# Mamba and mixture-of-experts layer on one core: the experts' rows are gathered plain and added by TensorE, where the gathering DMA added them before

## The reference

```python
x = L0_attn_x
xn = _layernorm(x)
x = x + attn(xn) + moe(xn)

# attn, for each direction (the backward one on the reversed sequence):
delta = softplus(dt @ dt_w.T + dt_b);  A = -exp(A_log)
h = h * exp(delta[..., None] * A) + (delta * xi)[..., None] * B[:, None, :]   # step by step over 512 tokens
y = einsum('bdn,bn->bd', h, C);  y = (y + xi * D) * silu(z);  out = y @ out_w.T
# moe, for the expert e that a token's router picks (argmax of 8 logits):
ye = (silu(xe @ gate_w[e].T) * (xe @ up_w[e].T)) @ down_w[e].T
```

## Time and profile before

| what | value |
|---|---|
| median of 3 runs | 995.46 us (993.8 to 995.51) |
| the profiled execution's own time | 996.43 us |
| its span, first to last instruction | 994.3 us |
| mean granted TensorE clock | 0.892 of full speed |
| busy: PE, DVE, ACT, POOL | 822.7, 889.1, 701.4, 817.0 us |
| POOL busy in 200 to 300, 600 to 700, 800 to 850, 900 to 950 us | 95.28, 88.43, 47.70, 47.70 us |
| DVE busy in 200 to 300, 600 to 700, 800 to 850, 900 to 950 us | 87.81, 92.22, 50.00, 40.84 us |
| ACT busy in 800 to 850, 900 to 950 us | 31.01, 26.02 us |

### The profile page before, as it was taken

One profiled execution on the slowest core, in us unless ns is written; L12 is line 12 of the kernel. 1 busy time (PEld: TensorE's weight loads), 2 busy tenths in 40 slices (PEclk: granted clock), 3 DMA queues, 4 the chain that ended last, 5 costly groups with the idle time before them and its releaser, 6 DMA issues.

```text
span 994.3 us, 10532 instructions
## 1 busy us (share of the span) xinstructions
PE 822.7 (83%) x2923; PEld 326.5 (33%) x2923; DVE 889.1 (89%) x622; ACT 701.4 (71%) x1167; POOL 817.0 (82%) x451
## 2 busy tenths in 40 slices
PE   5769886876869998989998998989998987676666
PEld 2223321132233543435343533435343321213112
DVE  4788979997899898999999897999989999895996
ACT  3877864746659789787998788788998584574440
POOL 0258767999999879897998878898888999999992
PEclk9778977797988999989999998989898897787779
DMA  6576262333273527464464626454453634634300
GB/s 193 155 200 177 54 183 54 143 88 92 102 187 138 131 65 217 117 192 112 148 173 144 138 76 202 121 173 128 142 151 85 156 59 124 141 115 95 69 1 11
DMA packets 93996, 125.54 MB, mean 126 GB/s; under 512 B 8042, under 2 KB 65771, under 8 KB 89843
## 3 DMA queue, kind: packets, MB, share of 16 engines
q1 hardware_dynamic: 88464, 120.15, 43.5%
q0 software_dynamic: 4736, 4.20, 2.1%
q10 hardware_dynamic: 738, 0.53, 0.2%
HBM read 77.53 MB, written 14.29 MB: 92 GB/s over the span
## 4 chain that ended last, share of the span: by engine, by line
PE 34%; POOL 29%; issue 17%; ACT 12%; DVE 3%; DMA 3%; SPq 1%; POOLq 0%; ACTq 0%; DVEq 0%
POOL hs L1250 18%; PE y L575 9%; PE front L513 6%; PE in_b L551 4%; POOL attn_in L1240 4%; POOL sorted_tokens L1221 3%; ACT dA L862 3%; ACT L871 3%; PE moe L696 2%; PE front L544 2%; PE front L526 2%; POOL yg L1212 2%; PE front L608 2%; PE moe L649 2%; PE moe L654 1%
## 5 line engine op out<-in xcount | busy, mean ns | idle before, releaser
L1250 POOL TENSOR_TENSOR hs<-hs,C_rep 128x1024 f32<-128x1024 f32 x252 | 595.4, 2416 | 123.0 <-DVE hs L1053 76.7
L862 ACT ACTIVATE dA<-delta_rep,A_sb 128x511 f32<-128x511 f32 x512 | 335.1, 715 | 66.3 <-DMA delta_rep<-tmpA 38.4
L1036 DVE TENSOR_TENSOR in_b<-in_b,B_rep 128x1024 f32<-128x1024 f32 x256 | 300.2, 1218 | 68.1 <-PE in_b L551 63.4
L575 PE MATMUL y<-hs,cst 128*32 128x512 f32 x1024 | 283.5, 681 | 46.7 <-POOL hs L1250 24.1
L1053 DVE TENSOR_TENSOR_SCAN hs<-dA,in_b 128x1024 f32<-128x1024 f32 x128 | 285.1, 2268 | 4.9 <-PE y L575 4.9
L1055 DVE TENSOR_TENSOR_SCAN hs<-dA,in_b 128x1024 f32<-128x1024 f32 x128 | 285.1, 2268 | 2.9 <-PE y L575 2.7
L551 PE MATMUL in_b<-du,cst 128*128 128x512 f32 x256 | 147.9, 662 | 24.7 <-DVE hs L1055 22.1
L513 PE MATMUL front<-xpad,w_in 128*128 128x512 f32 x248 | 124.9, 629 | 5.3 <-ACT zs L799 2.1
L575 PEld LDWEIGHTS y<-hs,cst 128*32 128x32 f32 x1024 | 53.5, 119 | 228.3 <-issue 177.7
L871 ACT ACT_TABLE_LOAD x73 | 93.7, 1283 | 14.1 <-PE moe L696 5.0
L544 PE MATMUL front<-dbc,w_dt 8*128 8x512 f32 x62 | 43.8, 792 | 37.3 <-ACT tmpB L825 19.4
(11 more groups left out here) (129 smaller groups left out, 771.6 us busy)
## 6 DMA issues: line engine op xcount, KB each, us to landing
delta_rep<-tmpA SPq DMA_DIRECT2D x126, 256.0 KB, 4.5
B_rep<-dbc_scratch SPq DMA_DIRECT2D x16, 1024.0 KB, 5.1
C_rep<-dbc_scratch SPq DMA_DIRECT2D x16, 1024.0 KB, 7.4
gu_w<-in_gate_up SPq DMA_DIRECT2D x39, 384.0 KB, 3.4
dn_w<-in_down SPq DMA_DIRECT2D x39, 192.0 KB, 2.5
xs<-sorted_tokens SPq DMA_DIRECT2D x39, 64.0 KB, 3.3
sorted_ffn<-ys SPq DMA_DIRECT2D x39, 64.0 KB, 1.6
sorted_tokens<-up_f SPq DMA_DIRECT2D x9, 256.0 KB, 4.1
```

What stands on the lines that cost most here:

```text
L575: i = e.matmul(Y[c * DD:(c + 1) * DD, :], sel, hs[:, (m + 2 * w + rh) % NH, r * L:(r + 1) * L], start=False, stop=(rh == 1 and r == RH - 1 ...
L862: i = e.activation(dA[:, m // 2 % NA, r * L + 1:(r + 1) * L], src, ACT.Exp, scale=A_sb[:, d, 2 * p + jj, r:r + 1])
L1036: e.tensor_tensor(to, in_b[:, 2 + 2 * odd, :].unsqueeze(1).broadcast_to([P, RH, L]), by, ALU.mult).then_inc(dve_mult, 1)
L1250: e.tensor_tensor(hs[:, m % NH, :], hs[:, m % NH, :], C_rep[:, u % 2, RH * rh:RH * rh + RH, :].rearrange("p r t -> p (r t)"), ALU.mult).th ...
```

## The change

For the sequences 0 to 5 the indirect DMAs no longer add. They write plain rows into half `b % 2` of `gu_w`, which the experts no longer need. TensorE puts the stored sum (`attn_in`) through the identity into the bank `M`, adds the gathered rows in the same way (`final_mm`, at step `g + 6`), and ScalarE copies `M` back into `attn_in` (at step `g + 7`), from where SP stores it as before (at step `g + 8`, now behind ScalarE's copy and not behind the gathers). GpSimd's gather no longer waits for the load of the stored sum, but from `b` = 2 on for the TensorE addition of `b - 2`.

```diff
+        def rows_of(b):
+
+            return gu_w[:, b % 2, :, :].rearrange("p a c -> p (a c)")[:, 0:KB * H].rearrange("p (k h) -> p k h", h=H)
+
...
                 for b in gathers(m, 8):
                     if b < NB - LATE:
-                        e.wait_ge(in_gather[b % 2], 64 * (b // 2 + 1))
+                        e.wait_ge(act_fin, b + 1)
                         e.dma_start(by_batch(out, b), attn_in[:, b % 2, :, :]).then_inc(out_fin[b % 2], 16)
...
+            def final_mm(b):
+
+                if b:
+                    e.wait_ge(act_fin, b)
+                else:
+                    e.wait_ge(act_ys, NTILE)
+                    e.wait_ge(act_up, NTILE)
+                e.wait_ge(in_attn[b % 2], 16 * (b // 2 + 1))
+                e.matmul(M[:, :], ident, attn_in[:, b % 2, :, :].rearrange("p k h -> p (k h)"), start=True, stop=False)
+                e.wait_ge(in_gather[b % 2], 64 * (b // 2 + 1))
+                e.matmul(M[:, :], ident, rows_of(b).rearrange("p k h -> p (k h)"),
+                         start=False, stop=True).then_inc(pe_fin, 1)
...
+                for b in gathers(m, 6):
+                    if b < NB - LATE:
+                        final_mm(b)
                 for c in norms(m, 5):
                     router(c)
...
+                for b in gathers(m, 7):
+                    if b < NB - LATE:
+                        e.wait_ge(pe_fin, b + 1)
+                        e.copy(attn_in[:, b % 2, :, :].rearrange("p k h -> p (k h)"), M[:, :]).then_inc(act_fin, 1)
...
                     if i < 0:
-                        e.wait_ge(in_attn[b % 2], 16 * (b // 2 + 1))
+                        if b >= 2:
+                            e.wait_ge(pe_fin, b - 1)
...
                         if i < 0:
-                            e.indirect_dma_start(out=attn_in[:, b % 2, k, :], out_offset=None, in_=ffn_d, in_offset=at,
-                                                 compute_op=ALU.add).then_inc(in_gather[b % 2], 16)
+                            e.indirect_dma_start(out=rows_of(b)[:, k, :], out_offset=None, in_=ffn_d,
+                                                 in_offset=at).then_inc(in_gather[b % 2], 16)
```

More of the change, by code:

```diff
@@ L248, in mamba_moe_kernel @@
         pe_first, pe_du, pe_y, pe_out = sem("pe_first"), sem("pe_du"), sem("pe_y"), sem("pe_out")
-        pe_base, pe_late = sem("pe_base"), sem("pe_late")
+        pe_base, pe_late, pe_fin = sem("pe_base"), sem("pe_late"), sem("pe_fin")
         pe_route, pe_xs, pe_gate, pe_up, pe_down = sem("pe_route"), sem("pe_xs"), sem("pe_gate"), sem("pe_up"), sem("pe_down")
@@ L258, in mamba_moe_kernel @@
         act_xsT, act_ys = sem("act_xsT"), sem("act_ys")
-        act_route = sem("act_route")
+        act_route, act_fin = sem("act_route"), sem("act_fin")
         act_y, act_D, act_up, act_out = sem("act_y"), sem("act_D"), sem("act_up"), sem("act_out")
```

## The result

The changed kernel takes 979.47 us (median of 5 runs, 977.51 to 980.77), the kernel before 994.55 us in the same comparison (5 runs). The ratio is 0.9839, with a 95% interval of 0.9826 to 0.9851, which is 16.0 us less (14.8 to 17.3); the two medians by themselves differ by 15.1 us. The forecast was 13.2 us less. So the direction and the place were right, and the size was short by some 3 us.

A forecast was written before the change was run, and what follows sets the result against it. GpSimd was taken as the bound from first gather to C(250): 14.2 us saved less 1 us of loss, 13.2 us, so 995.46 becomes 982.3 us. Range 979 to 990.5; its low end allowed 2 us for VectorE's tail or the clock.

The forecast's parts named there:

- What bounds it: From the first gather to C(250), about 180 us, GpSimd bounds the kernel while VectorE keeps up.
- The price of the adding, 14.2 us: On GpSimd, four adding gathers take 7.17 us, plain ones 4.80; the 2.37 us difference, times 6, is saved.
- I take 1 us of loss (bounds 0 and 3): Between 795 and 850 us GpSimd, running earlier, would wait for VectorE's scans, losing 1 us of the gain.
- So the tail ... moves by the full 14.2 us: The tail hangs on when GpSimd runs dry and moves 14.2 us earlier with it.
- behind each stand decay factors: ScalarE's six copies of 0.59 us delay only factors VectorE needs four steps later; cost 0.
- The wait at sequence 3: TensorE's second matmul waits for rows landing at 851.3; the sum starts 1.3 us later, VectorE's scans at 864.9.
- The wait at sequence 5: Rows land at 908.4, TensorE's second matmul ends at 910.5; VectorE loses 3 us, its later pair starts about 918.7.
- The slack at C(250): VectorE may start its pair by 920.0 without delaying GpSimd; estimated at 918.7, so 1.3 us remain.
- The end of C(251): VectorE's last multiplication ends about 954.6, again 1 us after GpSimd's last one.
- Rivals 1 and 2: VectorE becomes the bound, gain 5.4 to 10 us, chance 0.22; or final_mm holds TensorE at every gather, slower, 0.11.
- Rival 3: Gathers cost what they did, time 995 to 996 us; chance 0.05, shared with a stall just eating the gain.

The follow-up runs named there:

- Run 1: Changed kernel, but its gathers add again, onto the weights' buffer; matmuls, copy and waits kept. Ratio to the kernel before 0.9992.
- run 2: Kernel before with plain gathers onto attn_in, no new matmuls or copies, stored sum of sequences 0 to 5 lost. Ratio 0.9867.
- run 3: The change for sequences 0, 1 and 2 alone; 3, 4, 5 keep the adding DMA. Ratio to the kernel before 0.9936.
- Run 5: Kernel before with four unread identity matmuls filling TensorE's idle time ahead of the last sums of states. Ratio 0.9983.
- runs 3 and 4: The change for sequences 0, 1, 2 alone (ratio to the kernel before 0.9936), and for sequences 3, 4, 5 alone (0.9909).
- Runs 9 to 11: Changed kernel with VectorE gating y: three halves; six with additions at g + 8; six with additions at g + 6. Ratios 0.9844, 0.9888, 0.984.
- run 8: Changed kernel with TensorE's additions two steps earlier (g + 4) and ScalarE's copies at g + 5. Ratio to the kernel before 0.9913.

## Why the forecast was right in kind and short in size

**What bounds it: right.** In no profile of the two kernels does GpSimd wait for a scan between the first gather and C(250), and the two halves of the change shorten the middle part by 7.0 and 7.1 us, which add up to the whole.

**The price of the adding, 14.2 us: right.** 14.22 us measured in the middle part, blocks of four at 4.78 us where 4.80 were taken from the rows of another buffer. Run 1 shows that it is the adding.

**"I take 1 us of loss (bounds 0 and 3)": wrong, it was 0.** This is the first term that failed. I read the piece of 0.94 us called "issue" at 825.19 as a wait for a scan. It was none: the waits of GpSimd in the kernel before, in 788 to 968 us, name DMA issues alone. "Issue" in the chain is time in which the profile shows nothing to wait for; GpSimd was at work in it, since its records of five multiplications cover 814.57 to 826.74 without a break. After, the same five multiplications take 11.59 us, and no scan is late for them.

**"So the tail ... moves by the full 14.2 us": wrong by 1.6 us.** This is the larger of the two terms that failed, and it was missing from the sum rather than mis-sized: only the low bound of the range allowed 2 us for VectorE's tail or the clock, with no path worked out. The start of the tail moved as said, but its length did not stay. What the runs showed, over all profiles without filler: where VectorE came to C(251) about 4.2 us or more before GpSimd ran dry (before, run 2, run 3), TensorE idled for 3.6 to 4.6 us ahead of the last sums and these took 5.3 to 5.5 us. Where it came 0.2 to 2.2 us before (all others), TensorE idled for at most 1.3 us and they took 3.63 us. Run 5 shows the second half of this link by itself. The first half, that VectorE's lateness holds TensorE's spreads back and so brings its work close to the last sums, is read from the traces and was not tried alone. In the changed kernel it is the additions and their copies that make VectorE late, as runs 1 and 2 have it, and by runs 3 and 4 those of the sequences 3 to 5. The two terms make 2.6 of the 2.8 us between the forecast and the measured 16.0.

**ScalarE's copies, "behind each stand decay factors": wrong for sequence 4, though at no cost in the middle part.** The forecast had no term for the addition of sequence 4. These are ScalarE and, below, TensorE in the changed kernel (start us, us, idle before):

```profile
890.91 0.58 ACT L938 COPY attn_in<-moe 128x512 f32<-128x512 f32 x1 [3.66 <-PE moe L619]
891.39 0.59 ACT L819 COPY zs<-front 128x512 f32<-128x512 f32 x1
...
892.03 1.12 PE L591 MATMUL front<-comb_bias,ones 1*128 1x512 f32 x2 [1.16 <-ACT zs L819]
```

Behind the new copy stands the copy of `zs` that TensorE's bias matmul waits for, and ahead of the bias matmul stand the two new matmuls. GpSimd's gating was done at 886.47; the bias matmul came 5.6 us later and VectorE's pair of steps 236 and 237 11.2 us later, at 897.66. In run 2, without the additions, the same two distances are 0.7 and 8.0 us (gating done at 885.08, matmul at 885.80, pair at 893.07). These 3.2 us are what VectorE is later in the changed kernel at C(251) too: it comes there 1.0 us before GpSimd runs dry, in run 2 4.2 us. So the traces put the lateness that shortened the tail at sequence 4. No run has moved that addition alone.

**The wait at sequence 3: right.** Landing 6.3 us after the first start, as worked out. The scans behind it were put at 864.9 for a gather at 845.0; the gather started 1.1 us earlier than that and the scans, at 862.61, 2.3 us.

**The wait at sequence 5: right in its arithmetic, but not met.** The rows land at about 907.3. TensorE reached the second matmul only at 907.79, since it had been at work without a pause from that bias matmul on. So the price forecast here, 3 us, is 0. The pair that was said to start at 918.7 starts at 918.25, but by luck: a wait of 3 us that did not come made up for VectorE's pair at 897.66, forecast for 896, and for 0.6 us of idle time at the next.

**The slack at C(250): nearly right.** It was put at 1.3 us and was 0.9: VectorE's scan for it, the first of the pair at 946.96, was done at 949.2, and GpSimd began it at 950.1, one multiplication of 2.3 us before 952.41. Since the pair behind it was timed right by luck, this figure owes something to luck too. Runs 9 to 11 show it used up once GpSimd is 3.7 us earlier, and run 8 once VectorE is later.

**The end of C(251): right.** It ends at 953.49, 1.08 us after GpSimd ran dry at 952.41; in run 2 it took 5.28 us and ended at 952.13, 1.09 us after GpSimd. By the rule of the Trainium skill, SBUF — State Buffer, section "Who interferes with whom", a lock held for one instruction, run 2's should have had its turn when the one of GpSimd's five multiplications of 2.3 us ended that was running at its start. That was the fourth, and the fifth went ahead of it too. The traces do not agree with the rule in the kernel before (6.20 us) and in runs 2 (5.28), 3 (6.23) and 5 (6.22). In the changed kernel C(251) started within the fifth, which the rule allows.

**The rivals.** Rivals 1 and 2 did not come, though run 8 shows how near they were: two steps. Rival 3 fell with run 1.

## What to carry to other kernels

Price an edit by the block that it changes between other work, on the engine that is never idle there: six such blocks gave 14.2 us, and so did the middle part, which held to 0.2 us between the two profiles of the changed kernel (165.64 and 165.84 us), while its start moved by 4 us over all profiles. Ask of the engine behind the bound how far behind it is: here the saving of 14.2 us was kept in full. VectorE's scan for C(250) itself came 11.1 us earlier (958.08 to 946.96), since its idle time had hung on GpSimd, and the rest came out of its 5.0 us of slack. With 0.9 us of it left, the next saving of 3.7 us was worth nothing. And look at the last operations of the chain even if the edit is far from them: here their speed hung on how long TensorE had stood idle just before.

## What the runs showed of the hardware

An indirect DMA of 128 rows of 512 bytes that adds into SBUF holds GpSimd for 1.54 us, a plain one for 0.94 to 0.96 us, whichever of the buffers it writes (blocks of four: 7.2 and 4.8 us). Plain gathers landed 2.4 to 6.5 us after issue in the changed kernel (median 2.9), more spread than the plain ones of the kernel before showed. TensorE's last 16 records took 3.63 us at a granted clock of 1.00, and 5.3 to 5.5 us (at 0.66 to 0.68; the kernel before, runs 2 and 3) after 3.6 to 4.6 us of idle time, while up to 1.3 us of idle time left them at full speed. A VectorE multiplication with both inputs in SBUF, started 4.2 to 5.2 us before GpSimd had worked through its multiplications (the kernel before, runs 2, 3 and 5), took 5.3 to 6.2 us in place of 1.3 and ended about 1.1 us after GpSimd's last one, not after the one that was running.
